# A state-space layer and a butterfly FFN on one core: row halves in the output products, and a new order in VectorE's, ScalarE's and GpSimd's queues

## The reference

```
x = x + mamba(layernorm(x));   x = x + ffn(layernorm(x))

def mamba(x):                       # inner width 512, 16 states
    x_inner, z = split(x @ in_proj_w.T)
    xc = silu(causal_conv4(x_inner) + conv_b)
    dt, B, C = split(xc @ x_proj_w.T, [1, 16, 16])
    delta = softplus(dt);  A = -exp(A_log)
    h[t] = h[t-1] * exp(delta[t] * A) + xc[t] * delta[t] * B[t]
    y[t] = (h[t] * C[t]).sum(states) + xc[t] * D
    return (y * silu(z)) @ out_proj_w.T

def ffn(x):                         # hidden width 1024, 10 butterfly stages each way
    h = butterfly(x @ W_exp + b_exp, up_weights)
    h = gelu(h + up_bias)
    return butterfly(h, down_weights) @ W_con + b_con + down_bias
```

## Time and profile before

| | |
|---|---|
| time, median of 3 runs | 568.64 us (566.94 to 570.74) |
| profiled execution, its own time | 569.59 us |
| its span, first to last instruction | 567.87 us |
| granted TensorE clock, mean | 0.966 |
| busy: TensorE, VectorE, ScalarE, GpSimd | 528.9, 409.6, 306.1, 109.5 us |
| chain that ended last, by engine | PE 48%, DVE 20%, issue 12%, ACT 9%, SP's queue 6%, POOL 3% |

### The profile page before, as it was taken

How to read it: one execution, slowest core, us unless ns; L and a number is a source line. 1 busy time by engine, 2 the same in 40 slices (tenths; PEclk the granted TensorE clock), 3 DMA queues, 4 the chain that set the end, 5 groups by cost and what they waited for, 6 DMA issues and landing times.

```text
span 567.9 us, 8152 instructions
## 1 busy us (share of the span) xinstructions
PE 528.9 (93%) x2996; PEld 430.3 (76%) x2996; DVE 409.6 (72%) x860; ACT 306.1 (54%) x526; POOL 109.5 (19%) x96
## 2 busy tenths in 40 slices
PE   3998899888999999999999999999999999699896
PEld 3766676776897779887888778877888788578886
DVE  4859999587983799468966799379946894575532
ACT  2876883865239622874268623962287417431342
POOL 4042100230201301050103120130105021411110
PEclk9986979799999999999999999999999999799999
DMA  8542311200012001210112001200021002100011
GB/s 244 97 27 3 80 35 38 76 2 2 23 52 74 4 2 48 66 39 2 37 41 74 0 9 68 71 8 1 5 73 38 0 2 74 41 1 0 6 34 37
DMA packets 42619, 21.75 MB, mean 38 GB/s; under 512 B 26419, under 2 KB 41011, under 8 KB 42580
## 3 DMA queue, kind: packets, MB, share of 16 engines
q1 hardware_dynamic: 39940, 17.57, 13.0%
q10 hardware_dynamic: 2640, 3.67, 2.3%
HBM read 16.78 MB, written 4.46 MB: 37 GB/s over the span
## 4 chain that ended last, share of the span: by engine, by line
PE 48%; DVE 20%; issue 12%; ACT 9%; SPq 6%; POOL 3%; DMA 0%; DVEq 0%; ACTq 0%; POOLq 0%
PE wide L711 12%; PE acc L844 9%; PE wide L833 7%; SPq L420 5%; PE wide L822 4%; DVE xc L1552 2%; DVE xc L1555 2%; POOL x1b_xn L598 2%; DVE state L1516 2%; DVE hid_low L1429 2%; PE wide L804 2%; PE small L731 2%; PE wide L811 2%; DVE xc L1412 2%; ACT L1054 2%
## 5 line engine op out<-in xcount | busy, mean ns | idle before, releaser
L1054 ACT ACTIVATE hid_f<-wide,bias_up 128x512 f32<-128x512 f32 x64 | 44.0, 687 | 162.0 <-PE wide L833 161.6
L1412 DVE SCALAR_TENSOR_TENSOR xc<-xi,taps,xc 128x512 f32<-128x512 f32 x96 | 87.0, 911 | 4.0 <-ACT xc L1085 1.7
L844 PE MATMUL acc<-w_down_high,hid_high 128*128 128x256 f32 x256 | 73.2, 286 | 5.6 <-DVE hid_low L1429 5.4
L844 PE MATMUL acc<-w_down_high,hid_low 128*128 128x256 f32 x256 | 71.9, 281 | 0.0
L844 PE MATMUL acc<-w_down_low,hid_high 128*128 128x256 f32 x256 | 71.9, 281 | 0.0
L1429 DVE TENSOR_TENSOR hid_low<-hid_f,hid_high 128x512 fp32r<-128x512 f32 x64 | 46.3, 725 | 29.8 <-ACT hid_high L1163 29.2
L833 PE MATMUL wide<-xnT_ln2T_high,w_up_high 128*128 128x512 f32 x128 | 55.4, 432 | 3.4 <-DVE xnT_ln2T_low L1423 1.8
L522 POOL TENSOR_TENSOR rstd<-var_eps,minus_half 128x4 f32<-128x4 f32 x16 | 19.1, 1192 | 202.8 <-DVE var_eps L1317 202.8
L711 PE MATMUL wide<-xnT_ln1T_high,w_in_high 128*128 128x512 f32 x128 | 56.5, 441 | 1.1 <-DVE xnT_ln1T_low L1423 1.0
L822 PE MATMUL wide<-w_out,xc 128*128 128x256 f32 x256 | 56.7, 379 | 0.3 <-DVE xc L1555 0.3
L844 PEld LDWEIGHTS acc<-w_down_high,hid_high 128*128 128x128 f32 x256 | 48.0, 188 | 11.2 <-issue 8.2
(11 more groups left out here) (185 smaller groups left out, 1054.6 us busy)
## 6 DMA issues: line engine op xcount, KB each, us to landing
x_res<-in_L_attn_x_dram SPq DMA_DIRECT2D x9, 512.0 KB, 3.5
c_near<-c_of_tokens SPq DMA_DIRECT2D x8, 512.0 KB
out_dram<-x1b_xn SPq DMA_DIRECT2D x8, 512.0 KB, 2.9
x_ln<-in_L_attn_x_dram SPq DMA_DIRECT2D x7, 512.0 KB, 3.6
xc<-in_L_attn_in_proj_w_dram ACTq DMA_DIRECT2D x2, 512.0 KB, 7.1
xc<-in_L_ffn_W_exp_dram ACTq DMA_DIRECT2D x1, 1024.0 KB, 10.8
x1b_xn<-in_L_ffn_W_con_dram ACTq DMA_DIRECT2D x1, 1024.0 KB, 14.5
raw_out<-n_L_attn_out_proj_w_dram ACTq DMA_DIRECT2D x1, 512.0 KB, 7.0
```

The lines of the kernel that those rows point to most:

```text
L844: last = pe.matmul(acc[:, c, :], hid[h][:, j % HRING, c * P:(c + 1) * P], w_down[w][:, j, 0:DM], start=j == 0 and c % 2 == 0 and n == 0, s ...
L1054: ins = act.activation(out_ap, in_ap, how.pop("func"), **how)
L1412: ins = dve.scalar_tensor_tensor(xc[u % BATCH][:, e, :], xi[:, e, tap:tap + TILE], taps[:, e, tap:tap + 1], xc[u % BATCH][:, e, :], ALU.mu ...
```

## The change

1. **xd.** The two column halves of the x projection were added by a product with `fold`; now the sum is made when VectorE reads the transposed halves (a reduction of pairs), and TensorE only transposes.
2. **Diagonal.** The gaps product goes from GpSimd to VectorE, right behind the scan of gaps. GpSimd multiplies the spread C with B (`b_with_c`, in place in `c_near`) instead of the exponential with B, and does so after placing c_block; VectorE multiplies the exponential with that product.
3. **Outputs in row halves, from unit 2 on.** A bank now holds two channel blocks for half the tokens. The state product takes only the 64 rows that belong to that half: two products of 64 rows and 256 columns for one of 128 rows and 512. The second pair follows up 3 and down 1. Gates read half banks (four of 128x256) and then multiply whole blocks.
4. **VectorE's order from phase 2 on:** state, first low part of the FFN, then assembling; the second convolution block ahead of the gates.
5. **ScalarE:** the gelu table is loaded by an instruction of its own. In phase 7 high parts, gelus 0 to 2 and their up and down blocks stand among the light products.
6. **GpSimd:** the residual sum of unit u - 1 comes first in phase u, without waiting for the gates; the permutations of the set-up stand after the masks.
7. **Smaller:** in phase 0 the low parts of unit 2 ahead of the residual; in phase 1 up 2 ahead of the wait for w_down; the last FFN's final two down blocks, sum and store in halves.

```diff
+HALVES_FROM = 2
...
+    between = phase >= HALVES_FROM
-    WIDE_ORDER += uses(("up", range(3)), of=phase - 1) + uses(("y", range(CB)), of=phase)
-    WIDE_ORDER += uses(("up", range(3, 5)), of=phase - 1) + uses(("out", range(2)), of=phase)
+    WIDE_ORDER += uses(("up", range(3)), of=phase - 1) + uses(("y", range(2)), of=phase)
+    WIDE_ORDER += uses(("up", [3] if between else []), of=phase - 1) + uses(("y", range(2, CB)), of=phase)
+    WIDE_ORDER += uses(("up", [4] if between else [3, 4]), of=phase - 1) + uses(("out", range(2)), of=phase)
...
             for u in range(UNITS):
+                if u:
+                    residual_with_bias(u - 1)
                 weigh_gaps(u)
                 mask_b(u)
-                diagonal_gaps(u)
                 place_c_block(u)
-                diagonal_times_b(u)
+                b_with_c(u)
                 if u + 2 < UNITS:
                     rstd_of(u + 2, 0, var1, rstd1)
-                if u:
-                    wait(pool, gated, u, CB)
-                    residual_with_bias(u - 1)
                 rstd_of(u, 1, var2, rstd2)
...
-                    last = pe.matmul(bank[:, c * P:c * P + XD], xdT[:, c * P:(c + 1) * P], fold[:, :], start=True, stop=True)
+                    last = pe.transpose(bank[:, c * P:(c + 1) * P], xdT[:, c * P:(c + 1) * P], ident[:, :])
...
+            def ssm_output_halves(u, pair):
+
+                banks = [tile_of("y", 2 * pair + h, u) for h in range(2)]
+                for h in range(2):
+                    free(pe, u, "y", 2 * pair + h)
...
+                for q in range(2):
+                    g = 2 * pair + q
+                    for h in range(2):
+                        rows = slice(2 * SLOT * h, 2 * SLOT * (h + 1))
+                        last = pe.matmul(banks[h][:, q * HALF_TILE:(q + 1) * HALF_TILE],
+                                         state[u % BATCH][rows, g * P:(g + 1) * P],
+                                         c_startT[rows, h * HALF_TILE:(h + 1) * HALF_TILE],
...
+            def light_products_beside_ffn(u):
+
+                p = u - 1
+                up(p, 0)
+                up(p, 1)
+                step_sums(u)
+                up(p, 2)
+                decayed_b(u)
+                down(p, 0)
+                decayed_c_start(u)
+                decayed_c_block(u)
+                state_inputs(u)
+                down(p, 1)
+                off_diagonal(u)
...
+                    ssm_output_halves(u, 0)
+                    up(p, 3)
+                    if v < UNITS:
+                        down(p, 1)
+                    ssm_output_halves(u, 1)
...
+                for h in range(2):
+                    written(dve, u, "y", 2 * pair + h)
+                    tokens = slice(h * HALF_TILE, (h + 1) * HALF_TILE)
+                    for q in range(2):
+                        g = 2 * pair + q
+                        ins = dve.scalar_tensor_tensor(own[:, g, tokens], own[:, g, tokens], skip[:, g:g + 1],
+                                                       tile_of("y", 2 * pair + h, u)[:, q * HALF_TILE:(q + 1) * HALF_TILE],
+                                                       ALU.mult, ALU.add)
```

More of the change, by code:

```diff
@@ L53 @@
 SLOT = 32
+HALF_TILE = TILE // 2
 HALF = P // 2
@@ L492, in _ @@
                     load_for_residual(u + 1)
+                read(sp, u - 1, "down", 0)
                 store(u - 1)
-            store(UNITS - 1)
-            wait(sp, out_stored, UNITS - 1, 16)
+            sp.wait_ge(first_half_final, 1)
+            store(UNITS - 1, slice(0, GR // 2))
+            read(sp, UNITS - 1, "down", 0)
+            store(UNITS - 1, slice(GR // 2, GR))
+            wait(sp, out_stored, UNITS - 1, 2 * 16)
         @block.gpsimd
@@ L812, in ssm_output @@
                                                start=False, stop=True, skip_group_check=True), "y", g, u)
+            def ssm_output_halves(u, pair):
+                banks = [tile_of("y", 2 * pair + h, u) for h in range(2)]
+                for h in range(2):
+                    free(pe, u, "y", 2 * pair + h)
+                if pair == 0:
+                    read(pe, u, "moff", 0)
+                for q in range(2):
+                    g = 2 * pair + q
+                    for c in range(GR):
+                        at = q * HALF_TILE + c % 2 * P
+                        pe.matmul(banks[c // 2][:, at:at + P], x_tok[:, c, g * P:(g + 1) * P],
+                                  m_mat[:, c * P:(c + 1) * P], start=q == 0 and c % 2 == 0, stop=False,
+                                  skip_group_check=True)
+                if pair == 0:
+                    read(pe, u, "ct", 0)
+                    wait(pe, first_state, u, 1)
+                    wait(pe, states_ready, u, 1)
+                for q in range(2):
[5 more added lines that the diff above has]
+                                         c_startT[rows, h * HALF_TILE:(h + 1) * HALF_TILE],
+                                         start=False, stop=q == 1, skip_group_check=True)
+                        if q == 1:
+                            mark_written(last, "y", 2 * pair + h, u)
             def out_projection(u, h):
@@ L835, in up, with down @@
                 mark_written(last, "up", j, u)
-            def down(u, j):
+            def down(u, j, chunks=range(GR)):
                 if j == 0:
@@ L840, in down @@
                 wait(pe, hid_ready, u, j + 1)
-                for c in range(GR):
+                for c in chunks:
                     for n, (h, w) in enumerate(PASSES):
@@ L846, in down @@
                                          stop=j == HB - 1 and n == len(PASSES) - 1, skip_group_check=True)
+                if GR - 1 not in chunks:
+                    return last
                 if j == HB - 1:
@@ L962, in weights_of_ffn @@
                     prepare(17)
+                elif place == "up 2":
                     wait_all_taken("w_down")
@@ L966, in last_ffn @@
                 transposes(u, "ln2T", xn2, norm2)
-                for j in range(HB + 2):
-                    if j < HB:
-                        up(u, j)
+                for j in range(HB):
+                    up(u, j)
                     if j >= 2:
                         down(u, j - 2)
+                first, second = range(GR // 2), range(GR // 2, GR)
+                down(u, HB - 2, first)
+                down(u, HB - 1, first).then_inc(first_half_down, 1)
+                down(u, HB - 2, second)
+                down(u, HB - 1, second)
             prepare(0)
@@ L1214, in phase @@
                 beside("abs")
+                if v == UNITS:
+                    load_gelu_table()
+                    for j in range(3):
+                        gelu(p, j)
+                    load_exp_table(2)
                 if v < UNITS:
@@ L1665, in phase @@
                     convolve(v, 2)
+            def phase(u, beside=lambda place: None):
+                v, r, p = u + 1, u + 2, u - 1
+                take_xd(u)
+                if v == UNITS:
+                    low_parts(p, "ln2T")
+                softplus(u)
+                if v < UNITS:
+                    low_parts(p, "ln2T")
+                else:
+                    low_hidden(p, 0)
+                beside("softplus")
+                take_sums(u)
+                if v == UNITS:
+                    low_hidden(p, 1)
+                weigh(u)
+                weigh_b(u)
+                beside("weighed")
+                if u < HALVES_FROM:
+                    to_first_outputs(u, beside)
+                else:
+                    to_outputs_in_halves(u)
                 low_hidden(p, 4)
```

205 lines of the change are left out of this document (122 added, 83 removed).

## The result

| | before | after |
|---|---|---|
| median of 20 runs | 568.62 us | 566.12 us |
| profiled execution, span | 567.87 us | 564.9 us |
| granted TensorE clock, mean | 0.966 | 0.97 |

What follows compares the result with a forecast made beforehand. TensorE (busy 93%) was taken as the bound, VectorE as second limit inside a phase. Gains of 9.5 (steady phases), 0 (phases 0 and 1), 0 (phase 7) and 1.5 (end) sum to 11.0 us: about 558.5, range 551 to 565.

Steps and rivals of the forecast that it cites:

- Term 3: Steady phases 2 to 6, walking VectorE's queue: 1.9 us gained per phase, 9.5 in all; bounds per phase 1.0 and 3.2.
- Term 2: Output products in row halves, phases 2 to 7: TensorE saves 0.7 us per pair, 1.4 per phase.
- 1.0 per phase if halves run in line: Steady phases: row halves do not overlap, leaving 1.0 us gained per phase; one case within a rival of chance 0.17.
- Term 1: xd by four transposes instead of eight fold passes, every phase: 0.47 us for 0.91, TensorE saves 0.45.
- Term 4: Phases 0 and 1: freed bank and earlier up 2 against GpSimd's residual sum delaying normalising; taken 0, 2 lost to 4 gained.
- Term 5: Phase 7: later m_mat against TensorE work moved out of the way; taken 0, from 3 us lost to 3 gained.
- Term 6: The end: only half of the last sum and store stands there; 1.5 us gained, from 0.6 to 2.
- no-collision rival: Steady phases: GpSimd's product does not hold the first convolution; 3 us gained per phase, 551 to 555 in all; chance 0.22.
- The filling fails more than I count: Halves in line, softplus delay reaching TensorE, or phase 7 at the low clock: 563 to 566 us; chance 0.17.
- slower rival: Gates: half gates cost as much as whole ones, 0.78 us instead of 0.38; 5 us slower, 574; chance 0.05.

## Why the prediction was wrong, step by step

- **Term 3, steady phases: right.** 9.43 measured against 9.5, by the mechanism told: first convolution near 4.4, a stall at the first down block, gates at the second pair. After the x projection the walk had the first down block at 26.9 us, the two output groups at 28.3 and 34.7 and the output projection at 41.2; measured 26.75, 28.25, 34.4 and 41.25. That the sum came within 0.1 is partly luck: the first down block came 0.15 and the second group 0.3 earlier than walked, and row halves, which saved less than counted, took that back.
- **Term 2, row halves: mis-sized.** The passes stream together as forecast (eight starts in 1.06, forecast 1.0), but the changing over, put at 0.15 within that, adds about 0.4 per pair in all, as the starts around the passes show. Saved: 0.87 per phase instead of 1.4, of which 0.6 reaches the time. The price of the rival, "1.0 per phase if halves run in line", was near the 1.3 that is left without the 0.6.
- **Term 1:** the four transposes take 0.41 us to the next start in a steady phase (forecast 0.47); what of it reaches the time wasn't tried.
- **Term 4, phases 0 and 1: this step failed.** Taken 0, "from 2 lost to 4 gained"; measured 4.2 lost in the first profile and 1.1 to 4.2, mean 2.6, over the seven profiled executions with that beginning. The loss was told rightly: the residual sum holds the normalising, and behind it stand the softplus step, ScalarE's scaling and the first taps. What failed is what was set against it, the 2 us wait for the bank and the 1.4 of up 2 as gains. The wait did go, but TensorE ran on to the first tap, which became a wait of 3.2 us in one piece. And the low part that freed the bank stands ahead of the statistics, which begin 1.3 us later for it. Of the mean of 2.6, delta is 1.2 late and 1.6 is lost between delta and `m_mat`, where the granted clock was 0.50 for 3.4 to 10.2 us, a price that the term put at nothing; 0.3 comes back. By the medians and ratios, undoing either edit gives 2.4 to 3.9 us.
- **Term 5, phase 7: this step failed.** Taken 0, output projection 38.4 after the x projection; measured 43.2. Of the 4.8: 1.8 because the low clock of 483.0 to 486.4 fell on up 0 and 1, ahead of the third gelu; 1.5 because the passes after the 5.3 us wait took 3.55 us instead of 2.02 at half clock, which the prediction named ("1.5 to 3") and left out of the value taken; the remaining 1.5, not tried by itself, for waits on gates (0.31, 0.23) and blocks that the walk had packed without gaps. `m_mat` 4.7 later was 6.5. The first 1.8 is shown by the kernel with the first convolution late, whose last phase has the changed kernel's order and no low clock on up 0 and 1: `m_mat` is ready there after 28.4 us, where the walk had 28.35 and the changed kernel 30.2. The walk itself said that assembling behind the state costs 3.1 and the gelu 1.6, and I set against them a gain that needed the clock to hold.
- **Term 6, the end:** 0.95 for 1.5. Sum and store gave 0.54 and 0.8; the split of down 6 took 0.3 back.
- **Rivals.** The no-collision rival's price was too high by nearly all of it. "The filling fails more than I count", 563 to 566, is where the result nearly fell (566.1), but the number is luck: it counted 5 us for the steady phases, which gave 9.4, and 1 to 3 lost elsewhere, where 7.4 was lost. The halves did not run in line; phase 7 at the low clock was seen, but the reordered queues cost more. The slower rival did not occur.
- **The range.** Terms 4 and 5 had ranges of 6 us each and were both taken at zero. The bad end of both, 2 and 3 lost, gives 563.6; term 4 came out beyond it (4.2 in the first profile, 2.6 in the mean), and so did term 5 (3.2).

## What to carry to other kernels

A repeated phase can be forecast by walking two queues with durations from the trace. The first and last phases need their own walk, to the same depth, and a cost that the walk itself names, like passes at the low clock, belongs in the value taken and not only in the range. When a reordering removes a wait, look for the next instruction that isn't ready: the wait may only move there. Where the granted clock falls around it, add what the slow stretch costs (2.1 us for 6.8 here). An order that pays where an engine is full (state first, gelus early) can cost where it is empty; in a last phase put the result that others wait for first.

## What the runs showed of the hardware

- One moved call on VectorE gave 4.8 us for a 3.6 us earlier `m_mat`, most of the rest being sixteen passes of 2.02 us instead of 3.55, which ran at a granted clock of 0.50 behind a wait of 5.3 us. Behind waits of 2.2 us they took 2.02, 2.61, 2.79 and 3.48 in four kernels: a shorter wait does not by itself keep the clock.
- GpSimd's 128x1024 sum held VectorE whatever the size of VectorE's instruction: a 128x4 step took 2.17 us for 0.17, one of the four 128x256 normalisings 2.1 more, the gaps product of two broadcast inputs 3.24 for 1.22, while GpSimd's own took 2.34 to 2.40 us. In each GpSimd had begun first. In the kernel before, where VectorE's convolution began 0.16 us ahead of it, the same sum took 2.82.
- Row halves of the array stream side by side when their input rows and their banks are apart: two 64x256 passes start together every 0.216 us, where full-height passes of 256 columns start one by one at that pace. Changing over costs about 0.4 us per group of eight, so that 0.47 of the 0.86 is saved.
- The stretch from delta to `m_mat` of phase 1, with the gaps product on VectorE, took 23.0 us with no half clock in 97 to 125 us (five kernels), 23.4 with 3.4 us of it (two), 25.1 to 25.2 with 6.8 (five) and 26.15 with 10.2 (one).
